# A transformer block on one core: VectorE's middle of a pass in another order, and one product moved from VectorE to GpSimd

## Chip, cores and metric

One core of a Trainium2 chip runs the kernel. The metric is the device time of one execution in microseconds (us). The engines are TensorE (PE, with PEld for its weight loads), VectorE (DVE), ScalarE (ACT), GpSimd (POOL) and SyncE (SP, which issues DMAs here). Each runs its own instructions in order and waits on semaphores for the others.

## What is computed

An attention block and a mixture-of-ranks block, each with a layer norm before and after, on x of 16 x 256 x 128 (float32):

```python
x = x + layernorm(attention(layernorm(x)))    # 2 heads of 64, half of each head rotated (rope)
x = x + layernorm(ffn(layernorm(x)))

def ffn(x):                                   # for each row of 128
    base = x @ W.T
    proj = l2norm(x @ Wp.T + bp)
    lw = softmax(proj @ l2norm(sim) * exp(min(temp, CLAMP_MAX)))       # 4 experts
    ret = where(arange(4) == argmax(lw), lw, 0.0)                      # the best expert's weight alone
    return base + sum(ret[e] * ((x @ Wd[e].T) @ Wu[e].T) for e in range(4))   # ranks 1, 2, 4, 8
```

## The kernel before

The 16 batches go through as 8 pairs, n = 0 to 7 (LAST = 7). A pair is four tiles of 128 rows (t = 0 to 3), and four units u (two batches by two heads) in attention. All of x stays in SBUF. The main loop is `for a in PASSES` with a = 0 to 6. A pass works on several pairs at once: the attention of pair a (names `now`), the projections of pair a+1 (`nxt`), the statistics of pair a+3 (`has(a + 3)`), the second half of attention and the second norm of pair a-1 (`last_`), and the routing and low-rank part of pair a-2 (`done`). Behind the loop stands a tail written out by hand, with pair 5 (LAST-2) and 6 (LAST-1) to be finished and pair 7 (LAST) in halves.

Each engine has its own block with its own copy of the loop, and the order of calls in it is written out by hand. Nothing plans it. So each engine's order is fixed, and a call that waits holds up everything behind it on its engine.

What the change and the steps of the prediction touch:

- DVE, statistics of pair a+3: `stats` (L643, four times), `gap` (L649, L650), `mean` (L654, L655), `variance` (L659). They feed `norm_rows` (L266) and `norm_shift` on POOL in the next pass. `normalise(a+2)` (L664) writes two of the four tiles that TensorE's `turn_x(a+2)` (L1322) transposes; ACT writes the other two.
- DVE, attention: `row_max` (L675) of a unit's scores in PSUM, `weights_sum` (L680), `add_head` (L688), `residual_y` (L695) with the factor `rsy` from POOL (L297; in the tail L319). The four residuals of pair a-1 release TensorE's `turn_x2(a-1)` (L1383). `add_head(a, 0, .)` frees the PSUM bank that `turn_probs(a, 3)` writes.
- DVE, second norm: `stats_2` (L701), `gap_2`, `square_2`, `variance_2` (L716). They feed POOL's `deviation` (L309), the standard deviation `std2`. `scaled_bias` (L721) multiplies it with the routing bias, 4 x 62 elements for each of 128 partitions. `add_bias` (L727) adds it to what TensorE's `project_z` (L1395) left in PSUM. POOL's `scaled_guards` (L312, L313) make the small limits that `length` (L744) reads.
- DVE, routing of pair a-2: `top_logit`, `square_sum`, `length`, `below_top`, `keys` (L752), `top_key`, `logits` (L761; it needs `inv_norm` from POOL), `is_top`, `shares` (L769; it needs `expert_exps` of ACT, L463), `pick`, `sum_exps`, `invert_sum`, `gates` (L787, L789), `gates_low` (L794). TensorE's `turn_gated` (L1403) and `low_rank` follow, then ACT's `variance_z` (L474), POOL's `factors_z` (L303, L305: `rsz`) and DVE's `residual_z` (L799).
- POOL, in a pass: `inverse_lengths`, `factors_y`, `norm_rows(a+2)`, `rope(a+1, 0)`, `norm_shift`, `factors_z(a-2)`, `deviation(a-1)`, `rope(a+1, 1)`, `scaled_guards(a-1)`. `rope` is three products and sums of 256 elements (L282, L285, L288). It releases TensorE's `turn_qk(a+1, 0)` and `turn_qk(a+1, 1)` (L1341). The second of these stands at the start of the next pass, behind `weigh(a, 3)`; but that of the last pair stands in pass 6, ahead of `weigh(6, 3)`:

```python
                if nxt:
                    scores(a + 1, 0, (x2t_out, a) if last_ else (probs_ready, 4 * a + 3))
                if a == LAST - 1:
                    turn_qk(LAST, 1, (y_ready, 4 * a + 3))
                if now:
                    weigh(a, 3)
```

- ACT: `exps` (L438) needs `row_max` and makes the probabilities that `turn_probs` (L1362) transposes; `scores(a, 1)` (L1352) waits for the first two; `probs_copy` (L444), `variance_y` (L449), `qkt_copy` (L433), which copies what `turn_qk` wrote, and `gated_copy` (L467).

Of the kernel before, what the change touches and what calls it, by code (L numbers as in the profile page):

```python
# [16 lines left out]
P = 128  # L17
# [26 lines left out]
def layer(nc, x, w_attn, vectors, w_ffn, w_down, sim, out):  # L44
# [3 lines left out]
    with ctx:  # L48
# [192 lines left out]
        def _(pool):  # L241
# [68 lines left out]

            def scaled_guards(n):
                pool.tensor_tensor(eps2[:, n % 2, :], ve2[:, :], eps[:, :], ALU.mult)  # L312
                pool.tensor_tensor(least2[:, n % 2, :], ve2[:, :], tiny[:, :], ALU.mult).then_inc(least_ready, 1)  # L313
# [34 lines left out]
            for a in PASSES:  # L348
                if has(a - 2):
                    inverse_lengths(a - 2)  # L350
                if has(a - 1):
                    factors_y(a - 1)
                if a == 0:
                    pool.wait_ge(post_link, 2)
                    pool.tensor_tensor(sim_n[:, :], sim_sq[:, :], power[0:PROJ, 0:EXPERTS], ALU.pow).then_inc(sim_norm, 1)
                if has(a + 2):
                    norm_rows(a + 2)
                if has(a + 1):
                    rope(a + 1, 0)
                if has(a + 2):  # L360
                    norm_shift(a + 2)
                if has(a - 2):
                    factors_z(a - 2)
                if has(a - 1):
                    deviation(a - 1)
                if has(a + 1):
                    rope(a + 1, 1)
                if has(a - 1):
                    scaled_guards(a - 1)
# [4 lines left out]
            deviation(LAST - 1)  # L374
            scaled_guards(LAST - 1)
# [13 lines left out]
        def _(act):  # L389
# [136 lines left out]
            for a in PASSES:  # L526
# [11 lines left out]
                if has(a - 1):  # L538
                    variance_y(a - 1, 1)
                if now:  # L540
                    exps(a, 1)
                if done:
                    expert_exps(a - 2)
# [73 lines left out]
        def _(dve):  # L617
# [101 lines left out]
            def scaled_bias(n):  # L719
                dve.wait_ge(std_ready, n + 1)  # L720
                dve.tensor_tensor(bias_s[:, :, :], bias_b[:, :].unsqueeze(1).to_broadcast([P, PT, RW]),  # L721
                                  std2[:, :].unsqueeze(2).to_broadcast([P, PT, RW]), ALU.mult).then_inc(scaled, 1)

# [35 lines left out]
            def logits(n):  # L759
                dve.wait_ge(inv_norm_ready, n + 1)  # L760
                dve.tensor_tensor(logit[:, :, :], below[:, :, :], rank_wide(inv_norm), ALU.mult).then_inc(logits_ready, 1)  # L761
# [306 lines left out]
            for a in PASSES:  # L1068
# [32 lines left out]
                if done:  # L1101
                    keys(a - 2)
                if has(a + 3):
                    stats(a + 3, 0)
                if done:
                    top_key(a - 2)
                    logits(a - 2)
                    is_top(a - 2)
                if has(a + 3):
                    stats(a + 3, 1)  # L1110
                    stats(a + 3, 2)
                if done:
                    shares(a - 2)
                    pick(a - 2)
                if has(a + 3):
                    stats(a + 3, 3)
                if done:
                    sum_exps(a - 2)
                if last_:
                    residual_y(a - 1, 0)  # L1120
                if done:
                    invert_sum(a - 2)
                if has(a + 3):
                    gap(a + 3)
                if done:
                    gates(a - 2)
                if has(a + 3):
                    mean(a + 3)
                if done:
                    gates_low(a - 2)  # L1130
                if has(a + 3):
                    variance(a + 3)
                if now:
                    row_max(a, 2)
                if last_:
                    residual_y(a - 1, 1)
                    residual_y(a - 1, 2)
                if now:
                    row_max(a, 3)
# [11 lines left out]
                if last_:  # L1151
                    residual_y(a - 1, 3)
# [12 lines left out]
                if last_:  # L1165
                    variance_2(a - 1)
                if done:
# [11 lines left out]
                if last_:  # L1179
                    scaled_bias(a - 1)  # L1180
# [51 lines left out]
            scaled_bias(LAST - 1)  # L1232
# [392 lines left out]
```

## Time and profile before

| | us |
|---|---|
| median of 3 runs | 150.67 (150.66 to 150.72) |
| the profiled execution | 150.58 |
| its span in the trace | 148.80 |
| TensorE busy | 128.5 (86%) |
| VectorE busy | 130.7 (88%) |
| ScalarE busy | 113.4 (76%) |
| GpSimd busy | 87.3 (59%) |

The page gives each engine's busy time, and then the chain of work that ended last: TensorE has 49% of it, VectorE 27%, ScalarE 15%. A group or a timeline row names the line of the kernel, the engine, the operation, output and inputs with their shapes, and how many instructions are merged in it. A bracket behind it is the idle time of the engine ahead of it and what ended that. PE instructions overlap, so the time that one takes in its engine is the distance of two starts.

### The profile page before, as it was taken

How to read it: one execution, taken by the hardware profiler on the slowest of the kernel's cores; microseconds unless marked ns; L12 is line 12 of the kernel's file. 1: busy time of each engine (PE TensorE's matmuls, PEld its weight loads, DVE VectorE, ACT ScalarE, POOL GpSimd, SP SyncE). 2: the span in 40 equal slices, each digit the busy share in tenths (PEclk: the TensorE clock that was granted, in tenths of full speed). 3: DMA queues.
4: the chain of work that ended last, by engine and by line, in shares of the span. 5: the costliest groups of instructions: out<-in, count | busy, mean ns of one | idle time of the engine just before them, and what ended most of it. 6: DMA issues, size and time to landing. Idle time of an engine off the chain costs nothing.

```text
span 148.8 us, 3110 instructions
## 1 busy us (share of the span) xinstructions
PE 128.5 (86%) x874; PEld 106.0 (71%) x874; DVE 130.7 (88%) x592; ACT 113.4 (76%) x378; POOL 87.3 (59%) x148
## 2 busy tenths in 40 slices
PE   0879799999999998999899989998999898965340
PEld 0467587988898788878887888797879776953220
DVE  6788879997988999899989998898889788899963
ACT  3657697969996989698969896989698958754460
POOL 6320826623846758676867686768545863338552
PEclk9999999999999999999999999999999999999555
DMA  3833250000000000100020002000200010000013
GB/s 74 209 98 92 74 134 5 4 0 0 7 0 2 0 0 4 70 0 2 4 73 0 0 0 75 0 0 0 73 4 2 9 62 0 4 0 2 0 70 141
DMA packets 5266, 4.83 MB, mean 32 GB/s; under 512 B 594, under 2 KB 5250, under 8 KB 5250
## 3 DMA queue, kind: packets, MB, share of 16 engines
q1 hardware_dynamic: 5104, 4.51, 10.4%
q8 instruction: 7, 0.11, 0.3%
q10 hardware_dynamic: 146, 0.13, 0.3%
q14 instruction: 9, 0.07, 0.2%
HBM read 2.54 MB, written 2.10 MB: 31 GB/s over the span
## 4 chain that ended last, share of the span: by engine, by line
PE 49%; DVE 27%; ACT 15%; issue 2%; POOL 2%; DMA 2%; POOLq 1%; DVEq 0%
PE ps_a L1372 6%; PE ps_s L1352 6%; ACT probs L438 6%; PE ps_z L1395 5%; PE ps_c L1372 4%; DVE neg_max L675 4%; PE ps_a L1362 4%; DVE x_all L695 3%; PE ps_b L1322 2%; PE ps_s L1383 2%; PE ps_s L1341 2%; PE ps_b L1362 2%; DVE y_all L688 2%; DMA x_all<-x 2%; PE ps_c L1341 2%
## 5 line engine op out<-in xcount | busy, mean ns | idle before, releaser
L438 ACT ACTIVATE probs<-ps_s,neg_max 128x256 f32<-128x256 f32 x60 | 25.3, 488 | 7.9 <-DVE neg_max L675 7.8
L675 DVE TENSOR_REDUCE neg_max<-ps_s 128x2 f32<-128x512 f32 x30 | 20.3, 680 | 0.6 <-PE ps_s L1352 0.4
L1352 PE MATMUL ps_s<-qk_t 64*128 64x256 f32 x120 | 17.0, 402 | 0.0
L1372 PE MATMUL ps_a<-v_all,probs_t 128*128 128x129 f32 x120 | 16.5, 280 | 0.0
L1372 PEld LDWEIGHTS ps_a<-v_all,probs_t 128*128 128x128 f32 x120 | 14.6, 191 | 2.0 <-issue 2.0
L1352 PEld LDWEIGHTS ps_s<-qk_t 64*128 64x128 f32 x120 | 10.3, 186 | 4.8 <-issue 4.0
L282 POOL TENSOR_TENSOR turn<-qk,sin_x 128x256 f32<-128x256 f32 x15 | 11.1, 740 | 3.1 <-ACT qk L424 2.2
L695 DVE SCALAR_TENSOR_TENSOR x_all<-y_all,rsy,x_all 128x128 f32<-128x128 f32 x32 | 11.8, 393 | 1.3 <-POOL rsy L297 0.7
L285 POOL TENSOR_TENSOR qk<-qk,cos_x 128x256 f32<-128x256 f32 x15 | 11.5, 767 | 1.2
L297 POOL TENSOR_TENSOR rsy<-var_y,power 128x4 f32<-128x4 f32 x6 | 6.5, 1078 | 9.3 <-ACT sq_y L449 9.3
L293 POOL TENSOR_TENSOR inv_norm<-norm,power 128x4 f32<-128x4 f32 x7 | 7.2, 1027 | 8.0 <-DVE norm L744 8.0
L288 POOL TENSOR_TENSOR qk<-qk,turn 128x256 f32<-128x256 f32 x15 | 10.9, 725 | 1.2
L266 POOL TENSOR_TENSOR rs<-ve,power 128x4 f32<-128x4 f32 x7 | 7.1, 1008 | 6.2 <-DVE ve L659 6.2
L449 ACT ACTIVATE sq_y<-y_all 128x129 f32<-128x129 f32 x32 | 10.1, 339 | 0.7 <-DVE y_all L688 0.6
L309 POOL TENSOR_TENSOR std<-ve,root 128x4 f32<-128x4 f32 x7 | 7.1, 1017 | 5.3 <-DVE ve L716 5.3
L1362 PE MATMUL ps_a<-ident,probs 128*128 128x128 f32 x60 | 9.1, 275 | 1.1 <-ACT probs L438 1.1
L444 ACT ACTIVATE probs_t<-ps_a 128x512 f32<-128x512 f32 x15 | 9.5, 637 | 0.5 <-PE ps_a L1362 0.5
L1395 PE MATMUL ps_z<-w_z,x_t 128*128 128x190 f32 x48 | 9.5, 325 | 0.0
L1362 PEld LDWEIGHTS ps_a<-ident,probs 128*128 128x128 f32 x60 | 7.0, 140 | 2.6 <-ACT probs L438 1.6
L1372 PE MATMUL ps_c<-v_all,probs_t 128*128 128x129 f32 x64 | 8.6, 278 | 0.2 <-ACT probs_t L444 0.2
L799 DVE SCALAR_TENSOR_TENSOR x_all<-ps_z,rsz,x_all 128x128 f32<-128x128 f32 x24 | 7.3, 342 | 1.4 <-POOL rsz L305 1.4
L1372 PE MATMUL ps_b<-v_all,probs_t 128*128 128x129 f32 x64 | 8.5, 276 | 0.0
(342 smaller groups left out, 442.0 us busy)
## 6 DMA issues: line engine op xcount, KB each, us to landing
x_all<-x SPq DMA_DIRECT2D x7, 256.0 KB, 2.8
out<-x_all SPq DMA_DIRECT2D x7, 256.0 KB, 2.1
x_all<-x SPq DMA_DIRECT2D x2, 128.0 KB, 2.7
out<-x_all SPq DMA_DIRECT2D x2, 128.0 KB, 1.7
w_raw<-w_attn ACTq DMA_DIRECT2D x1, 128.0 KB, 2.8
w_raw<-w_attn SPq DMA_DIRECT2D x1, 128.0 KB, 2.9
bo_bp<-vectors SPq DMA_DIRECT2D x1, 80.0 KB, 3.5
ffn_raw<-w_ffn SPq DMA_DIRECT2D x1, 71.5 KB
```

The source lines that it names most:

```text
L282: pool.tensor_tensor(turn[:, b, :, :, :], swapped, sin_x[:, :, :, :, :].rearrange("p t g h i -> p (t g) h i"), ALU.mult).then_inc(rope_mid, 1)
L285: pool.tensor_tensor(spatial, spatial, cos_x[:, :, :, :, :].rearrange("p t g h i -> p (t g) (h i)"), ALU.mult).then_inc(rope_mid, 1)
L288: pool.tensor_tensor(spatial, spatial, turn[:, b, :, :, :].rearrange("p g h i -> p g (h i)"), ALU.add).then_inc(rope_done, 1)
L438: last = act.activation(probs[:, u, j, :], scores_of(n, u)[:, j * T:(j + 1) * T], ACT.Exp, bias=neg_max[:, u, j:j + 1])
L444: act.activation(probs_t[:, u, :, :], unit_of(n, u)[:, :].rearrange("p (a t) -> p a t", a=TILES), ACT.Copy).then_inc(pt_out, 1)
L449: last = act.activation(sq_y[:, t, :], y_all[:, n * PT + t, :], ACT.Square, scale=E ** -0.5, accum_out=var_y[:, t:t + 1])
L675: dve.tensor_reduce(neg_max[:, u, :], scores_of(n, u)[:, :].rearrange("p (j k) -> p j k", j=TILES), AX.X, ALU.max, negate=True).then_inc(m ...
L695: dve.scalar_tensor_tensor(x_all[:, rows(n, t)], y_all[:, n * PT + t, 0:E], rsy[:, t:t + 1], x_all[:, rows(n, t)], ALU.mult, ALU.add).then ...
L1352: last = pe.matmul(scores_of(n, 2 * b + h)[:, j * T:(j + 1) * T], qk_t[r, b, 0, j * P:(j + 1) * P], qk_t[r, b, 1, :], start=True, stop=True)
L1362: last = pe.transpose(unit_of(n, u)[:, i * T + j * P:i * T + (j + 1) * P], probs[:, u, j, i * P:(i + 1) * P], ident[:, :])
L1372: last = pe.matmul(unit_of(n, u)[:, j * VW:(j + 1) * VW], probs_t[:, u, i, j * P:(j + 1) * P], v_all[:, at:at + VW], start=(i == 0), stop= ...
L1395: last = pe.matmul(z_of(n, k)[:, t, :], x2_t[:, 2 * k + t, :], w_z[:, :], start=(t == 0), stop=False, skip_group_check=True)
```

## The change

On POOL, `scaled_bias` is new: the same product, with `bias_s` as its output, behind `deviation`, in each pass from a = 1 and once in the tail. It waits for POOL's own `std_ready`, and for the `add_bias` of the pair before (`route_ready`), which read the tile. The same function and its two calls are gone from DVE. On ACT `expert_exps(a-2)` goes ahead of `exps(a, 1)`. On DVE the middle of a pass has another order: `logits` ahead of `keys`, the routing operations and the statistics interleaved otherwise, `row_max(a, 2)` and `row_max(a, 3)` next to each other, then `residual_y` 1, 2 and 3 of pair a-1 in a row, and `mean` and `variance` of pair a+3 behind `variance_2`, ahead of `residual_z` and `normalise`. TensorE's order stays as it is.

```diff
@@ GpSimd
+            def scaled_bias(n):
+                pool.wait_ge(std_ready, n + 1)
+                if n == 0:
+                    pool.wait_ge(post_dve, 5)
+                else:
+                    pool.wait_ge(route_ready, 2 * n)
+                pool.tensor_tensor(bias_s[:, :, :], bias_b[:, :].unsqueeze(1).to_broadcast([P, PT, RW]),
+                                   std2[:, :].unsqueeze(2).to_broadcast([P, PT, RW]), ALU.mult).then_inc(scaled, 1)
...
                 if has(a - 1):
                     deviation(a - 1)
+                    scaled_bias(a - 1)
                 if has(a + 1):
                     rope(a + 1, 1)
...
             deviation(LAST - 1)
+            scaled_bias(LAST - 1)
             scaled_guards(LAST - 1)
@@ ScalarE
+                if done:
+                    expert_exps(a - 2)
                 if now:
                     exps(a, 1)
-                if done:
-                    expert_exps(a - 2)
@@ VectorE
                 if done:
+                    logits(a - 2)
                     keys(a - 2)
                 if has(a + 3):
                     stats(a + 3, 0)
                 if done:
                     top_key(a - 2)
-                    logits(a - 2)
-                    is_top(a - 2)
                 if has(a + 3):
                     stats(a + 3, 1)
+                if done:
+                    is_top(a - 2)
+                    shares(a - 2)
+                if has(a + 3):
                     stats(a + 3, 2)
                 if done:
-                    shares(a - 2)
                     pick(a - 2)
+                    sum_exps(a - 2)
                 if has(a + 3):
                     stats(a + 3, 3)
                 if done:
-                    sum_exps(a - 2)
+                    invert_sum(a - 2)
                 if last_:
                     residual_y(a - 1, 0)
                 if done:
-                    invert_sum(a - 2)
+                    gates(a - 2)
                 if has(a + 3):
                     gap(a + 3)
                 if done:
-                    gates(a - 2)
-                if has(a + 3):
-                    mean(a + 3)
-                if done:
                     gates_low(a - 2)
-                if has(a + 3):
-                    variance(a + 3)
                 if now:
                     row_max(a, 2)
+                    row_max(a, 3)
                 if last_:
                     residual_y(a - 1, 1)
                     residual_y(a - 1, 2)
-                if now:
-                    row_max(a, 3)
+                    residual_y(a - 1, 3)
+                if now:
                     weights_sum(a, 0)
...
                 if last_:
-                    residual_y(a - 1, 3)
                     stats_2(a - 1, 2)
                     stats_2(a - 1, 3)
...
                 if last_:
                     variance_2(a - 1)
+                if has(a + 3):
+                    mean(a + 3)
+                    variance(a + 3)
                 if done:
                     residual_z(a - 2, 0)
...
-                if last_:
-                    scaled_bias(a - 1)
                 if now:
                     add_head(a, 2, 0)
...
             add_head(LAST, 2, 1)
-            scaled_bias(LAST - 1)
             weights_sum(LAST, 3)
```

## Rows read from the trace of the kernel before

**Rows 1.** Windows: a pass with statistics, one without; busy time of each engine, clock, DMA
```profile
60.79:75.70 14.91, 14.30 (x108) 12.18 (x106) 14.43 (x64) 12.96 (x46) 10.62 (x17) 1.00 0.06 19
90.60:105.44 14.84, 14.29 (x108) 12.17 (x106) 12.86 (x54) 12.90 (x46) 10.80 (x18) 1.00 0.06 20
```

**Rows 2.** Timeline of TensorE, pass 3: start, us, engine, line, operation, idle before
```profile
71.24 0.66 PE L1383 MATMUL ps_s<-ident,x_all 128*128 128x128 f32 x4 [0.61 <-DVE x_all L695]
```

**Rows 3.** Timeline of TensorE, pass 5: `turn_probs(2)`, `turn_x2`, `turn_probs(3)`
```profile
99.83 0.60 PE L1362 MATMUL ps_c<-ident,probs 128*128 128x128 f32 x4
100.27 0.60 PE L1383 MATMUL ps_s<-ident,x_all 128*128 128x128 f32 x4
101.41 0.66 PE L1362 MATMUL ps_a<-ident,probs 128*128 128x128 f32 x4 [0.55 <-ACT probs L438]
```

**Rows 4.** Timeline of POOL, pass 3: two of the three operations of `rope(4, 0)`
```profile
66.59 0.74 POOL L282 TENSOR_TENSOR turn<-qk,sin_x 128x256 f32<-128x256 f32 x1
67.40 0.74 POOL L285 TENSOR_TENSOR qk<-qk,cos_x 128x256 f32<-128x256 f32 x1
```

**Rows 5.** Timeline of DVE, pass 3: `mean`, `variance`; then all `mean` (ns: min/median/max)
```profile
66.62 0.73 DVE L654 SCALAR_TENSOR_TENSOR mean<-tmp,stats 128x4 f32<-128x4 f32 x1
...
67.47 0.69 DVE L659 SCALAR_TENSOR_TENSOR ve<-tmp 128x4 f32<-128x4 f32 x1
...
L654 DVE SCALAR_TENSOR_TENSOR mean<-tmp,stats x7: 165/168/726, 14.3 to 81.5; 128x4 f32<-128x4 f32 x7
```

**Rows 6.** Costliest groups: last sum of `rope`; then tile `bias_s` (ns: min/median/max)
```profile
L288 POOL TENSOR_TENSOR qk<-qk,turn 128x256 f32<-128x256 f32 x15 | 10.9, 725 | 1.2
...
L721 DVE TENSOR_TENSOR bias_s<-bias_b,std x7: 394/515/827, 44.0 to 130.8; 128x248 f32<-128x248 f32 x7
```

**Rows 7.** Timelines of POOL and DVE, start of pass 4: second guard, `length`
```profile
76.07 0.21 POOL L313 TENSOR_TENSOR least<-ve,tiny 128x4 f32<-128x4 f32 x1
...
77.21 0.15 DVE L744 TENSOR_TENSOR norm<-norm,least 128x4 f32<-128x4 f32 x1
```

**Rows 8.** Timelines, end of pass 6: `deviation`, last sum of `rope(7, 1)`, `turn_qk(7, 1)`, its copy
```profile
116.80 1.02 POOL L309 TENSOR_TENSOR std<-ve,root 128x4 f32<-128x4 f32 x1
...
119.46 0.72 POOL L288 TENSOR_TENSOR qk<-qk,turn 128x256 f32<-128x256 f32 x1
...
120.51 0.66 PE L1341 MATMUL ps_c<-ident,qk 128*128 128x128 f32 x4
...
121.21 0.60 ACT L433 ACTIVATE qk_t<-ps_c 128x512 f32<-128x512 f32 x1 [0.95 <-PE ps_c L1341]
```

**Rows 9.** Timelines of POOL and DVE, tail: `deviation(6)`, first operation of `gates(5)`
```profile
128.25 1.01 POOL L309 TENSOR_TENSOR std<-ve,root 128x4 f32<-128x4 f32 x1 [2.38 <-DVE ve L716]
...
129.78 0.22 DVE L787 TENSOR_TENSOR gate<-picked,total 128x60 f32<-128x60 f32 x1
```

**Rows 10.** Pass 0: `normalise(2)`, all of them; `rope(1, 1)`, first and last; `turn_x(2)`
```profile
28.66 1.38 DVE L664 TENSOR_SCALAR xn<-x_all,rs,nm 128x128 f32<-128x128 f32 x2
...
L664 DVE TENSOR_SCALAR xn<-x_all,rs,nm x12: 333/341/886, 28.7 to 102.8; 128x128 f32<-128x128 f32 x12
...
28.41 0.74 POOL L282 TENSOR_TENSOR turn<-qk,sin_x 128x256 f32<-128x256 f32 x1 [1.09 <-ACT qk L424]
...
30.04 0.72 POOL L288 TENSOR_TENSOR qk<-qk,turn 128x256 f32<-128x256 f32 x1
...
30.68 0.66 PE L1322 MATMUL ps_b<-ident,xn 128*128 128x128 f32 x4
```

**Rows 11.** Pass 1: TensorE's `turn_probs(2)`, `turn_x2`; DVE's `residual_y` 1 and 2
```profile
40.78 0.60 PE L1362 MATMUL ps_c<-ident,probs 128*128 128x128 f32 x4
41.41 0.66 PE L1383 MATMUL ps_s<-ident,x_all 128*128 128x128 f32 x4
...
38.45 1.08 DVE L695 SCALAR_TENSOR_TENSOR x_all<-y_all,rsy,x_all 128x128 f32<-128x128 f32 x2
```

**Rows 12.** Timeline of POOL, pass 1: `deviation(0)`
```profile
42.77 1.06 POOL L309 TENSOR_TENSOR std<-ve,root 128x4 f32<-128x4 f32 x1 [2.14 <-DVE ve L716]
```

More of the change, by code:

```diff
@@ L716, in variance_2 @@
                 dve.scalar_tensor_tensor(ve2[:, :], tmp2[:, 1, :], 1.0 / E, tmp2[:, 2, :], ALU.mult, ALU.add).then_inc(var2, 1)
[L719 to L722, printed above, removed]
             def add_bias(n, k):
@@ L760, in logits @@
                 dve.wait_ge(inv_norm_ready, n + 1)
+                dve.wait_ge(route_link, n * 9 + 3)
                 dve.tensor_tensor(logit[:, :, :], below[:, :, :], rank_wide(inv_norm), ALU.mult).then_inc(logits_ready, 1)
```

## The prediction

> **What bounds the kernel now.** I read the page first (the busy shares and the chain that ended last), then TensorE's timeline over two whole passes, then the timelines of VectorE (DVE), ScalarE (ACT) and GpSimd (POOL) beside it, and last the start, pass 1 and the tail, where the steady state doesn't hold. A pass (one value of a in the main loop) lasts 14.91 us where four more statistics, a mean and a variance lie in it (a = 2 to 4), and 14.84 us without them (a = 5) [rows 1]. TensorE is busy 14.30 and 14.29 us of these. So DVE's 14.43 busy us against 12.86 are worth only 0.07 us a pass: TensorE's order is the floor. In passes 2 to 4 TensorE waits 0.61 us for the last `residual_y` ahead of `turn_x2` [rows 2]. In pass 5 it doesn't: `turn_x2` follows `turn_probs(2)` after 0.44 us, and TensorE then waits 0.55 us for `exps(a, 3)` on ACT ahead of `turn_probs(3)` [rows 3]. ACT gets there from `gated_copy`, `exps(2)` and `variance_z`, all released by TensorE itself. Whoever frees DVE's middle finds this second wait behind the first.
>
> **DVE's middle (gain).** `mean` takes 0.73 us and `variance` 0.69 us in pass 3 and the median `mean` of all passes 0.17 [rows 5]. Both lie beside a product of `rope` on POOL and end with it: 66.59 + 0.74 = 67.33 against 66.62 + 0.73 = 67.35, and 67.40 + 0.74 = 68.14 against 67.47 + 0.69 = 68.16 [rows 4, 5]. Both read two SBUF operands. The change takes them out of the middle, joins the two maxima (PSUM operands, not held up) and puts `residual_y` 1 to 3 in a row behind. By these rows the middle loses about 1.2 us, and the last residual is ready about 1.1 us ahead of TensorE even if two of the three are held by a product of `rope`. The 0.61 us wait goes, the 0.55 us wait of pass 5 comes: a gain of 0.07 us in each of the passes 2, 3 and 4, **-0.21 us**. Passes 5 and 6 gain nothing. `logits` ahead of `keys` and `expert_exps` ahead of `exps(a, 1)` have one answer: `exps(a, 1)` ends some 0.2 us later, its reader `scores(a, 1)` has more slack than that, **0**. `mean` and `variance` at the end fall, in passes 2 to 4, into DVE's wait for `rsz`, beside a power on POOL: **0**. The cover is that wait, and pass 0 has none.
>
> The Trainium skill (SBUF — State Buffer, section "Who interferes with whom") says that a VectorE instruction with two SBUF inputs contends with a GpSimd instruction that reads SBUF, and that the later one fully blocks. By that rule, the trace agrees (the two ends above). It speaks for moving `mean` and against giving POOL one more product: without it the tail term below would lose 0.1 us and the pass 0 term would be 0.
>
> **The product on POOL (its price).** No POOL row has this shape (248 elements, both operands broadcast). The nearest is a product or sum of 256 elements, 725 ns in the mean over 15 [rows 6]: 0.70 us for 248, plus 0.08 us for the wait on POOL's own `std_ready` (the distance of dependent POOL instructions, as 66.59 + 0.74 to 67.40 [rows 4]): **0.78 us**. Bounds: 0.39 us, what DVE takes for it at the least, and 1.1 us, half as much again. On DVE 0.39 to 0.83 us go [rows 6], where it isn't late: in each pass and in the tail DVE waits next for TensorE's `project_z(., 1)`. So the removal alone is worth **0**. What is queued behind the product on POOL is `rope(a+1, 1)` and `scaled_guards(a-1)`; who waits for these is TensorE's `turn_qk(a+1, 1)` and DVE's `length`.
>
> In steady passes: the guards end at 76.07 + 0.21 = 76.28 and `length` reads them at 77.21 [rows 7]. They come at most 0.78 us later; POOL also starts `deviation` a little earlier (DVE's `variance_2` is earlier, so only `rsz` holds it): 0.15 to 0.4 us are left. **0**, with a cliff from about 1 us of product.
>
> In pass 6, the last, there is no such slack. `turn_qk(LAST, 1)` stands right behind `scores(LAST, 0)`, at 120.51, and `rope(LAST, 1)` ends at 119.46 + 0.72 = 120.18 [rows 8]. `deviation` starts there at 116.80 behind `rsz`, which ACT releases, so it can't be earlier. Now `rope` ends at 120.96, TensorE starts at 121.02 (0.06 us of a semaphore): **+0.51 us**. It is handed on: ACT has waited 0.95 us for just this operation [rows 8], the copy feeds `scores(LAST, 1)`, and the chain of waits runs from there over TensorE and ACT to the end without a gap of more than 0.3 us.
>
> In the tail the product runs from 128.25 + 1.01 + 0.08 = 129.34 to 130.04, and `gates` (two SBUF operands) comes at 129.78 [rows 9]; it ends at about 130.1 and not at 130.0, and the chain runs through it: **+0.1 us**.
>
> **Pass 0.** `mean(3)` and `variance(3)` now stand right ahead of `normalise(2)`, and `rope(1, 1)` runs beside it, from 28.41 to 30.04 + 0.72 = 30.76. There the two instructions of `normalise` together take 1.38 us, one of them 886 ns where the median is 341; so they too are held up by POOL [rows 10]. Now: `mean` is held to 29.15 by the first product; `variance`, 0.2 us behind, is held by the second to 29.96; the first `normalise` slips in between; the second is held by the third to about 30.9 instead of 30.04. TensorE's `turn_x(2)` stood at 30.68: **+0.28 us**. DVE itself, which has a short wait for TensorE behind, is about 0.6 us late, and so are the maxima and exponentials that open pass 1.
>
> **Pass 1.** Alone it would gain: `turn_x2` came 0.63 us behind `turn_probs(2)`, not 0.44 [rows 11], so -0.19. But DVE comes 0.6 us late; the second and third residual meet two products of `rope` (that pair took 1.08 us before [rows 11], with a maximum behind it), and now stand in a row ahead of `add_head(1, 0, .)`, which frees the bank for `turn_probs(3)`. I work that out to 42.2, where TensorE was free at 41.41 + 0.44 = 41.85. So passes 0 and 1 together: **+0.31 us** (an estimate, rounded down for the colder start that `turn_x2` had). `variance_2` is then 0.8 us later and `deviation` starts at 43.6 instead of 42.77 [rows 12]. In pass 6 `rope` ends 3.4 us behind the start of `deviation` (116.80 to 120.18 [rows 8]); with the product and two guards of 0.2 us that makes about 48.1 for the guards of pass 1. `length` of pass 2 would come two passes ahead of that in [rows 7], at 77.21 - 29.82 + 0.31 = 47.7. So DVE waits 0.4 us, and the copies on ACT hand perhaps 0.16 us of it to TensorE (bounds 0 and 0.4, taken low as the second exponential has slack): **+0.16 us**.
>
> **Sum.** -0.21 + 0.51 + 0.10 + 0.31 + 0.16 = +0.87 us on the profiled execution, 150.58 us (span 148.80), so 151.45; the median of the runs shown is 0.09 above it: 151.5 us, 0.6% slower.
>
> **Rivals.**
> 1. The start keeps its time (DVE's `normalise` finds a gap between POOL's products, or wins the second race). For it: instructions of this kind do slip between two products; against it: the 1.38 us of the pair there. Passes 0 and 1 give -0.19 and pass 2 nothing: -0.19 - 0.21 + 0.61 = +0.21, 150.9 us, within 0.2%. 20 in 100.
> 2. The faster side: POOL's product is cheap (near 0.39 us) or starts early, `rope(LAST, 1)` stays at most 0.1 us behind TensorE, and the start keeps its time: -0.40 + 0.2 = 150.5, down to 150.3 us with nothing left in the tail. It decides below 0.27 us of product and wait together (0.33 less a semaphore); no row speaks for that. 11 in 100.
> 3. The product takes 1.1 us or more on POOL: the tail pays 0.4 us more, and the guards come behind `length` in all of the passes 2 to 6, at up to 0.1 us each: 152.1 us. 12 in 100.
> 4. The change doesn't do what it says: `turn_x2` still waits for DVE in passes 2 to 4, as the three residuals are held longer than a product each. Then the -0.21 is missing: 151.7 us. 7 in 100, within the range of the forecast.
>
> The forecast has 50 in 100, from 151.2 to 151.8. About 0.2% (0.3 us) is what a measurement of this kernel can tell from no change. Slower by more than that (over 150.97): forecast, rivals 3 and 4 and a little of rival 1, 70 in 100. Within 0.2%: most of rival 1 and half of rival 2, 20. Faster: 10. The range of 8 in 10 leaves out the far end of rivals 2 and 3: 150.5 to 152.1.
>
> **What would show each step.** In the changed kernel: TensorE's wait ahead of `turn_x2` gone and 0.5 us ahead of `turn_probs(3)` in passes 2 to 4, which last 14.84 us; `mean` at 0.17 us there; POOL's new product at 0.70 us, 7 times; ACT's wait ahead of the copy for `scores(LAST, 1)` at 1.4 to 1.5 us instead of 0.95, with TensorE idle ahead of `turn_qk(LAST, 1)` for 0.5 us; in pass 0 `mean` and `variance` at 0.5 to 0.7 us and a wait ahead of `turn_x(2)`; in pass 2 POOL's guards behind DVE's `length`. The prediction is wrong if passes 2 to 4 come out shorter than 14.8 us, or if `turn_qk(LAST, 1)` isn't late.

## The result, and the profile after

The changed kernel takes 151.23 us (151.13 to 151.33) where the kernel before took 150.71 us (150.5 to 150.76) beside it on the same chip: ratio 1.0036, 95% interval 1.0027 to 1.0046. It is slower by 0.52 us. The profiled execution took 151.26 us, 0.68 us more than that of before.

The page after, parts 1 and 4 (busy time of each engine, then its share of the chain that ended last):

```profile
PE 129.2 (86%) x874; PEld 106.5 (71%) x874; DVE 128.9 (86%) x585; ACT 113.0 (76%) x378; POOL 90.0 (60%) x155
...
PE 57%; DVE 16%; ACT 15%; POOL 5%; issue 3%; DMA 2%; POOLq 1%; DVEq 0%
```

VectorE lost 1.8 us of busy time and went from 27% of the chain to 16%; POOL went from 87.3 to 90.0 us busy and now has 5% of the chain. Yet the kernel is slower.

One mark for each pass shows where: the start of `scores(a, 0)` on TensorE, the same instruction in both kernels (us from the start of the span).

| start of | before | after | pass lasts, before | after | difference |
|---|---|---|---|---|---|
| pass 0 | 15.31 | 15.45 | | | +0.14 (ahead of anything that was changed) |
| pass 1 | 31.27 | 31.69 | 15.96 | 16.24 | +0.28 |
| pass 2 | 45.49 | 46.03 | 14.22 | 14.34 | +0.12 |
| pass 3 | 60.41 | 60.86 | 14.92 | 14.83 | -0.09 |
| pass 4 | 75.32 | 75.69 | 14.91 | 14.83 | -0.08 |
| pass 5 | 90.22 | 90.52 | 14.90 | 14.83 | -0.07 |
| pass 6 | 105.06 | 105.36 | 14.84 | 14.84 | 0 |
| `scores(7, 0)` | 119.45 | 119.74 | 14.39 | 14.38 | -0.01 |
| `turn_qk(7, 1)` | 120.51 | 121.18 | 1.06 | 1.44 | +0.38 |

The column of differences adds up to +0.67 us, with 0.14 of it in the loading phase (in the experiments below this start lies between 15.10 and 15.51, whatever was changed); the rest agrees with the 0.52 us between the medians.

**The steady passes.** Windows of the kernel after, pass 3 and pass 5 (borders, length; busy time of PE, PEld, DVE, ACT, POOL; granted clock, DMA), to be laid beside [rows 1]:

```profile
60.86:75.69 14.83, 14.28 (x105) 12.16 (x104) 13.76 (x61) 12.92 (x46) 10.91 (x18) 1.00 0.06 19
90.52:105.36 14.84, 14.30 (x106) 12.17 (x105) 13.03 (x52) 12.93 (x46) 10.92 (x18) 1.00 0.05 18
```

VectorE has 0.67 us less to do in pass 3, and the pass is shorter by 0.08 us: the two kinds of pass are now alike. TensorE's timeline, pass 3, the three rows that answer to [rows 2, 3]:

```profile
70.46 0.60 PE L1366 MATMUL ps_c<-ident,probs 128*128 128x128 f32 x4
70.90 0.60 PE L1387 MATMUL ps_s<-ident,x_all 128*128 128x128 f32 x4
...
72.05 0.66 PE L1366 MATMUL ps_a<-ident,probs 128*128 128x128 f32 x4 [0.55 <-ACT probs L449]
```

`turn_x2` follows `turn_probs(2)` after 0.44 us without a wait, and the wait is in its new place, 0.55 us for `exps(3)`.

**Pass 0.** Timelines of VectorE, POOL and TensorE after, to be laid beside [rows 10]:

```profile
28.80 0.52 DVE L665 SCALAR_TENSOR_TENSOR mean<-tmp,stats 128x4 f32<-128x4 f32 x1
29.42 0.70 DVE L670 SCALAR_TENSOR_TENSOR ve<-tmp 128x4 f32<-128x4 f32 x1
30.04 1.00 DVE L675 TENSOR_SCALAR xn<-x_all,rs,nm 128x128 f32<-128x128 f32 x2
...
28.55 0.74 POOL L282 TENSOR_TENSOR turn<-qk,sin_x 128x256 f32<-128x256 f32 x1 [1.10 <-ACT qk L435]
29.37 0.73 POOL L285 TENSOR_TENSOR qk<-qk,cos_x 128x256 f32<-128x256 f32 x1
30.18 0.78 POOL L288 TENSOR_TENSOR qk<-qk,turn 128x256 f32<-128x256 f32 x1
...
31.10 0.66 PE L1326 MATMUL ps_b<-ident,xn 128*128 128x128 f32 x4 [0.22 <-DVE xn L675]
```

Each operation of `rope` holds one step of VectorE, which ends only with it: `mean` ends at 29.32 with the first (28.55 + 0.74 = 29.29), `variance` at 30.12 with the second (30.10), `normalise` at 31.04 with the third (30.96). TensorE then waits 0.22 us.

**The end of pass 6.** Timelines of POOL and TensorE, then ACT, to be laid beside [rows 8]:

```profile
117.14 1.01 POOL L309 TENSOR_TENSOR std<-ve,root 128x4 f32<-128x4 f32 x1
118.23 0.60 POOL L317 TENSOR_TENSOR bias_s<-bias_b,std 128x248 f32<-128x248 f32 x1
...
120.40 0.72 POOL L288 TENSOR_TENSOR qk<-qk,turn 128x256 f32<-128x256 f32 x1
...
121.18 0.66 PE L1345 MATMUL ps_c<-ident,qk 128*128 128x128 f32 x4 [0.30 <-POOL qk L288]
...
121.87 0.60 ACT L444 ACTIVATE qk_t<-ps_c 128x512 f32<-128x512 f32 x1 [1.32 <-PE ps_c L1345]
```

TensorE now waits for POOL ahead of `turn_qk(7, 1)`, and ACT's wait behind it grew from 0.95 to 1.32 us. In the chain of waits POOL stands here from `std` to `qk` without a break.

### The profile page after: what moved, and what is told of

Read it like the earlier page. It is cut to its first block, busy times and chain, and to the rows that moved or that the text cites. A ratio compares the mean times of both kernels' runs of the same rounds, so it can differ in the third digit from the quotient of the medians.

```text
span 149.5 us, 3124 instructions
## 1 busy us (share of the span) xinstructions
PE 129.2 (86%) x874; PEld 106.5 (71%) x874; DVE 128.9 (86%) x585; ACT 113.0 (76%) x378; POOL 90.0 (60%) x155
## 4 chain that ended last, share of the span: by engine, by line
PE 57%; DVE 16%; ACT 15%; POOL 5%; issue 3%; DMA 2%; POOLq 1%; DVEq 0%
PE ps_a L1376 10%; PE ps_s L1356 9%; ACT probs L449 5%; PE ps_z L1399 4%; PE ps_a L1366 4%; ACT sq_z L485 3%; PE ps_b L1366 3%; PE ps_c L1376 3%; PE ps_c L1345 3%; PE ps_b L1326 2%; DMA x_all<-x 2%; DVE y_all L699 2%; PE ps_s L1345 1%; ACT gated_t L478 1%; PE ps_d L1333 1%
## 5 line engine op out<-in xcount | busy, mean ns | idle before, releaser
L686 DVE TENSOR_REDUCE neg_max<-ps_s 128x2 f32<-128x512 f32 x30 | 19.8, 683 | 1.6 <-PE ps_s L1356 1.4
L706 DVE SCALAR_TENSOR_TENSOR x_all<-y_all,rsy,x_all 128x128 f32<-128x128 f32 x32 | 13.5, 460 | 1.5 <-POOL rsy L328 0.8
L285 POOL TENSOR_TENSOR qk<-qk,cos_x 128x256 f32<-128x256 f32 x15 | 10.9, 730 | 1.2
```

What stands on the lines that cost most here:

```text
L285: pool.tensor_tensor(spatial, spatial, cos_x[:, :, :, :, :].rearrange("p t g h i -> p (t g) (h i)"), ALU.mult).then_inc(rope_mid, 1)
L686: dve.tensor_reduce(neg_max[:, u, :], scores_of(n, u)[:, :].rearrange("p (j k) -> p j k", j=TILES), AX.X, ALU.max, negate=True).then_inc(m ...
L706: dve.scalar_tensor_tensor(x_all[:, rows(n, t)], y_all[:, n * PT + t, 0:E], rsy[:, t:t + 1], x_all[:, rows(n, t)], ALU.mult, ALU.add).then ...
```

## The experiments

The theory is the prediction's: the reordering gains in the passes 1 to 4 and loses in pass 0 (and hands it to pass 1), and the product on POOL costs in the pass with no slack, pass 6. Against it stand, first, that the loss has one cause alone (the reordering, or POOL's queue in every pass), and second, that one wait is only exchanged for another, so that a repair of one place moves nothing. Each expectation says which it tells apart; a later question is how the gain of the steady passes comes about.

**1. The reordering alone.** The product is back on VectorE, the rest is the change.

```diff
@@ the changed kernel, GpSimd
-                    scaled_bias(a - 1)
...
@@ VectorE
...
+                if last_:
+                    scaled_bias(a - 1)
                 if now:
                     add_head(a, 2, 0)
...
```

> The new order on DVE and ACT alone; the product of deviation and routing bias stays on DVE, where the kernel before has it. Theory A (three places that add up: the start, where mean and variance meet rope ahead of normalise, +0.28 us in pass 0 and +0.12 in pass 1; passes 2 to 4, -0.08 each; the tail, +0.38 through the late rope of the last pair): +0.28 + 0.12 - 0.24 = +0.16 us over the kernel before, 150.87 us, and turn_qk(LAST, 1) not late. Theory B (the product on POOL is the whole loss, the order only gains): -0.4 to -0.25 us. Theory C (the order is the whole loss): +0.5 us.

Measured: 150.90 us, ratio 1.0015 (1.0006 to 1.0024), +0.25 us. In its trace the starts of the passes lie at 15.44, 31.66, 45.99, 60.81, 75.64, 90.46, 105.29 and 119.67, those of the full change within 0.07 us, but `turn_qk(7, 1)` comes 1.07 us behind the last of them, without a wait. TensorE's timeline, pass 6:

```profile
120.74 0.66 PE L1342 MATMUL ps_c<-ident,qk 128*128 128x128 f32 x4
```

So the loss of the start belongs to the reordering alone, and the loss of the end doesn't.

**2. The product on POOL alone**, in the order of before.

```diff
@@ the kernel before, GpSimd
                     deviation(a - 1)
+                    scaled_bias(a - 1)
...
@@ VectorE
...
-                if last_:
-                    scaled_bias(a - 1)
...
```

> The product on POOL alone; the order on DVE and ACT as before. Theory A: the tail's +0.38 us and nothing in pass 0; pass 1 and 2 at most 0.1 more, as variance_2 isn't late there: +0.4 us, 151.1 us. Theory B: +0.5 us or more, spread over the passes. Theory C: 0.

Measured: 151.08 us, ratio 1.0029 (1.0018 to 1.0041), +0.43 us. The starts of the passes (15.10, 31.11, 45.34, 60.22, 75.12, 90.02, 104.85, 119.23) give passes of 14.88 to 14.90 us with statistics, as before. The loss is at the end, 1.39 us from `scores(7, 0)` to

```profile
120.62 0.66 PE L1344 MATMUL ps_c<-ident,qk 128*128 128x128 f32 x4 [0.25 <-POOL qk L288]
```

The two parts alone add up to 0.68 us, the whole costs 0.52; the intervals of the two (about 0.15 us each) leave room for that.

**3. The product on VectorE in pass 6 only.** Undoes one call of the change.

```diff
@@ the changed kernel, GpSimd
-                    scaled_bias(a - 1)
+                    if a != LAST - 1:
+                        scaled_bias(a - 1)
@@ VectorE
...
+                if a == LAST - 1:
+                    scaled_bias(a - 1)
                 if now:
                     add_head(a, 2, 0)
```

> The changed kernel with the product back on DVE in pass 6 alone (6 of 7 products stay on POOL). Theory A: rope(LAST, 1) is on time, turn_qk(LAST, 1) follows scores(LAST, 0) without a wait, and 0.38 of the 0.52 us lost are back: +0.15 us over the kernel before, 150.85 us. Theory B (POOL's load in every pass): a sixth or a seventh of the loss comes back, under 0.1 us. Theory C: nothing comes back.

Measured: 150.83 us, ratio 1.0011 (1.0002 to 1.0020). Of the seven products on POOL this one cost 0.4 us (1.0036 less 1.0011, times 150.7), what `turn_qk(7, 1)` was late by; it now stands 1.07 us behind `scores(7, 0)` (119.73), without a wait:

```profile
120.80 0.66 PE L1353 MATMUL ps_c<-ident,qk 128*128 128x128 f32 x4
```

**4. `mean` and `variance` in the middle in pass 0 only.**

```diff
@@ the changed kernel, VectorE
                 if has(a + 3):
                     gap(a + 3)
+                if a == 0:
+                    mean(a + 3)
+                    variance(a + 3)
...
-                if has(a + 3):
+                if has(a + 3) and a > 0:
                     mean(a + 3)
                     variance(a + 3)
```

> The changed kernel with mean(3) and variance(3) of pass 0 back in the middle, behind gap(3); all later passes as changed. Theory A: normalise(2) is on time, turn_x(2) waits for nothing (-0.28 us), DVE isn't late in pass 1, turn_x2 is released in time there and the wait that the kernel before had goes (-0.3 us): 0.6 us under the changed kernel, 150.65 us, -0.05 us against the kernel before. Theory B: no change against the changed kernel (+0.5). Theory C (the order in the passes, wherever it stands): under 0.1 us comes back.

Measured: 150.62 us, ratio 0.9996 (0.9987 to 1.0004). Starts at 15.31, 31.23, 45.27, 60.10, 74.93, 89.75, 104.57, 118.96: pass 0 lasts 15.92 us, pass 1 14.04, together 0.62 us less than after the full change. So the place of two small instructions in one pass costs 0.6 us. VectorE and TensorE, pass 0:

```profile
28.66 1.35 DVE L675 TENSOR_SCALAR xn<-x_all,rs,nm 128x128 f32<-128x128 f32 x2
...
30.65 0.66 PE L1329 MATMUL ps_b<-ident,xn 128*128 128x128 f32 x4
```

`normalise` meets the products of `rope` as it did before ([rows 10]), and TensorE doesn't wait. Pass 1 also shows the gain that the late start had covered: 14.04 against 14.22 us before.

**5. Both repairs** (3 and 4 in one kernel).

> The changed kernel with both repairs: the product of pass 6 back on DVE, and mean(3) and variance(3) of pass 0 back in the middle. Theory A: the two losses are separate and add up: 0.4 us under the kernel with the second repair alone, 0.4 us under the kernel before, 150.25 us (ratio 0.997). If the two share a cause (both are POOL being late somewhere), less than 0.2 us comes on top of the better one of them.

Measured: 150.24 us, ratio 0.9973 (0.9964 to 0.9983), faster than before by 0.36 us. The starts from pass 2 on (45.27, 60.10, 74.93, 89.75, 104.58, 118.97) are those of experiment 4 within 0.01 us, so the two repairs don't touch each other. Neither wait was only exchanged for another: what each cost comes back whole.

**6. The product of pass 6 twice**, the first into a tile that is free then. It adds a product and takes nothing away.

```diff
@@ the changed kernel, GpSimd
                     deviation(a - 1)
+                    if a == LAST - 1:
+                        pool.wait_ge(std_ready, a)
+                        pool.tensor_tensor(bias_e[:, :, :], bias_b[:, :].unsqueeze(1).to_broadcast([P, PT, RW]),
+                                           std2[:, :].unsqueeze(2).to_broadcast([P, PT, RW]), ALU.mult)
                     scaled_bias(a - 1)
```

> The changed kernel with the product done twice on POOL in pass 6 alone (the first into a tile that is written anew later). Theory A: POOL's time ahead of rope(LAST, 1) goes to the end one for one: another 0.6 us, +1.1 us over the kernel before, 151.8 us; TensorE waits 0.9 us ahead of turn_qk(LAST, 1). If the 0.38 us were something else than this wait (the lock on DVE, ACT's late exponentials), under 0.2 us more.

Measured: 151.69 us, ratio 1.0070 (1.0057 to 1.0083). Against the changed kernel +0.5 us, and TensorE's wait went from 0.30 to 0.85 us, by about one product of 0.60:

```profile
121.48 0.66 PE L1349 MATMUL ps_c<-ident,qk 128*128 128x128 f32 x4 [0.85 <-POOL qk L288]
```

At this place each product on POOL goes straight to the end of the kernel.

**7. `mean` and `variance` at the end, nothing else** (from pass 1 on). This was to show the 0.07 us of the passes 2 to 4 alone, and the two held instructions as their cause.

```diff
@@ the kernel before, VectorE
                 if has(a + 3):
                     gap(a + 3)
...
-                if has(a + 3):
+                if a == 0:
                     mean(a + 3)
...
-                if has(a + 3):
+                if a == 0:
                     variance(a + 3)
...
                 if last_:
                     variance_2(a - 1)
+                if has(a + 3) and a > 0:
+                    mean(a + 3)
+                    variance(a + 3)
```

> The kernel before with one edit: from pass 1 on, mean and variance stand behind variance_2. No other reordering, no product on POOL. Theory A: the two held instructions are the whole of what keeps the last residual_y from TensorE, so this alone gives pass 1 its 0.2 us and passes 2 to 4 their 0.08 us each: -0.4 us, 150.25 us. Rival: the gain needs the maxima together and the three residuals in a row as well: -0.1 us at most.

A miss, with the sign wrong: 151.16 us, ratio 1.0035 (1.0023 to 1.0048). The passes 2 to 4 last 15.1 us (starts 45.69, 60.80, 75.93, 91.07), longer than before. VectorE's timeline, pass 3, with TensorE's `turn_x2` and `turn_x` and POOL's `rope` beside it:

```profile
67.14 0.66 DVE L794 TENSOR_TENSOR gated<-gate,gated 128x60 fp32r<-128x60 f32 x1
...
68.32 1.16 DVE L695 SCALAR_TENSOR_TENSOR x_all<-y_all,rsy,x_all 128x128 f32<-128x128 f32 x2
...
71.37 0.66 PE L1386 MATMUL ps_s<-ident,x_all 128*128 128x128 f32 x4 [0.36 <-DVE x_all L695]
...
74.57 0.66 PE L1325 MATMUL ps_b<-ident,xn 128*128 128x128 f32 x4
...
73.43 1.08 DVE L664 TENSOR_SCALAR xn<-x_all,rs,nm 128x128 f32<-128x128 f32 x2
...
73.71 0.72 POOL L282 TENSOR_TENSOR turn<-qk,sin_x 128x256 f32<-128x256 f32 x1
```

Most of the time that `mean` and `variance` were held stayed in the middle. `gates_low`, which took their place beside `rope`, now takes 0.66 us instead of 0.21, and two residuals 1.16 us instead of 0.67: that is 0.94 of the 1.2 us. The rest did arrive: the last residual ends 10.51 us after the start of the pass (71.31), where it ended 10.77 us after it before (71.18), and `turn_x2` waits for it for 0.36 us instead of 0.61. So the 0.2 us a pass were not lost in the middle but at the new place. There the two stand ahead of `residual_z` and `normalise`, though `rsz` is ready (at 72.58, before `variance` starts at 72.83), and they push `normalise` onto the next `rope`, beside which its pair takes 1.08 us (twice its 333 to 341 ns is 0.68, [rows 10]). It ends at 74.51, and TensorE's `turn_x`, which needs it, starts at 74.57.

**8. The maxima and residuals joined, nothing else.** This one is the opposite part: `mean` and `variance` stay where they were held.

```diff
@@ the kernel before, VectorE
                     row_max(a, 2)
+                    row_max(a, 3)
                 if last_:
                     residual_y(a - 1, 1)
                     residual_y(a - 1, 2)
+                    residual_y(a - 1, 3)
                 if now:
-                    row_max(a, 3)
                     weights_sum(a, 0)
...
                 if last_:
-                    residual_y(a - 1, 3)
                     stats_2(a - 1, 2)
```

> The kernel before with only the maxima joined and the three residuals in a row; mean and variance stay in the middle, held at 0.7 us each. Theory D: the held time costs nothing by itself as long as the last residual isn't behind the heads: it ends at about 70.1 in the clock of the trace of before, TensorE wants it at 70.5, so passes 2 to 4 fall to 14.84 us and the whole to 150.3 us (-0.3). Theory A (the two held instructions are the delay): the 1.2 us are still there, -0.1 us at most.

Measured: 150.29 us, ratio 0.9971 (0.9960 to 0.9982). A few moved lines of one engine beat both kernels, by 0.4 us the kernel before. The passes 2 to 5 last 14.82, 14.82, 14.83 and 14.82 us (starts 45.42, 60.24, 75.06, 89.89, 104.71), and pass 1 14.05 instead of 14.22. VectorE's timeline, pass 3, then TensorE's:

```profile
66.46 0.73 DVE L654 SCALAR_TENSOR_TENSOR mean<-tmp,stats 128x4 f32<-128x4 f32 x1
...
67.31 0.68 DVE L659 SCALAR_TENSOR_TENSOR ve<-tmp 128x4 f32<-128x4 f32 x1
67.92 1.28 DVE L675 TENSOR_REDUCE neg_max<-ps_s 128x2 f32<-128x512 f32 x2
69.11 0.86 DVE L695 SCALAR_TENSOR_TENSOR x_all<-y_all,rsy,x_all 128x128 f32<-128x128 f32 x3
...
70.28 0.60 PE L1383 MATMUL ps_s<-ident,x_all 128*128 128x128 f32 x4
...
71.42 0.66 PE L1362 MATMUL ps_a<-ident,probs 128*128 128x128 f32 x4 [0.54 <-ACT probs L438]
```

`mean` and `variance` are held just as before, 0.73 and 0.68 us, and it costs nothing: the last residual is ready at 69.97, 0.3 us ahead of TensorE. In the changed kernel it is ready at 69.82, 1.08 us ahead of TensorE (70.90), and the pass is no shorter: a residual that is in time gains nothing by being earlier. What made `turn_x2` wait in the kernel before is that the third residual stood behind a maximum and the first heads, not that the middle held two blocked instructions.

**9. `mean` and `variance` moved, maxima joined**, the product still on VectorE and the routing operations in the order of before; in pass 0 the two stay in the middle.

> The kernel with mean and variance moved alone (from pass 1 on), and now also row_max 2 and 3 next to each other and residual_y 1, 2 and 3 in a row behind them. Gates' chain, logits and expert_exps as in the kernel before, products on DVE. New theory D (what holds DVE is the run of three products of rope, whoever reads two SBUF operands then; what counts is that PSUM reads stand beside it and that the last residual comes ahead of the heads): turn_x2 in time, passes 2 to 4 at 14.84 us, -0.4 us, 150.2 us. Theory A': the gates' chain pulled forward is needed too: no gain against the kernel before, or a loss as with mean moved alone (+0.5).

Measured: 150.40 us, ratio 0.9977 (0.9968 to 0.9986), passes 14.82 and 14.83 us. No gain beyond experiment 8: with the residuals in a row, the place of `mean` is worth nothing, as its end is hidden either way.

**10. The whole reordering, no product on POOL, pass 0 repaired.** This asks what the product on POOL is worth where it does no harm.

> The new order with mean(3) and variance(3) of pass 0 in the middle, and every product on DVE as in the kernel before. Theory A: moving the product to POOL buys nothing in any pass, so this is as fast as the kernel with both repairs, 150.25 us, within 0.1 us. Rival: DVE's 0.4 us a pass, which the move frees, are worth something: slower than that kernel by 0.2 us or more.

Measured: 150.25 us, ratio 0.9974 (0.9962 to 0.9985), against 150.24 with six of the seven products on POOL (experiment 5). VectorE's relief is worth nothing, as the prediction had it.

**11. The second wait removed too.** On the kernel of experiment 10 ACT's `exps(a, 3)` goes ahead of `variance_z(a-2)`.

```diff
@@ the kernel of experiment 10, ScalarE
                     exps(a, 2)
-                if done:
-                    variance_z(a - 2)
                 if now:
                     exps(a, 3)
+                if done:
+                    variance_z(a - 2)
```

> The new order with every product on DVE and mean(3) in the middle of pass 0, and one more edit on ACT: exps(a, 3) ahead of variance_z(a-2), so that TensorE's 0.55 us wait ahead of turn_probs(3) goes. If that wait is what bounds passes 2 to 6, each gains up to 0.5 us (-2 us, 148 us). But variance_z comes 0.7 us later, and with it rsz, deviation, the product, add_bias and the guards: I expect DVE and POOL to be late next at the end of the pass, and 0.1 to 0.3 us a pass to be left: 149.0 us, 148.3 to 150.3.

A miss: 152.15 us, ratio 1.0097 (1.0081 to 1.0112), with passes of 15.12 to 15.16 us. The wait of 0.55 us is gone, and a longer way has opened. The chain of waits of this kernel, pass 3 (start, us, what):

```profile
70.69 1.04 ACT sq_z L474 x8
...
71.80 0.23 POOL var_z L303
...
72.09 1.03 POOL rsz L305
...
73.15 0.62 DVE x_all L800 x2
...
73.81 0.91 PE ps_z L1399 x4
```

`project_z(a-1, 0)` writes the bank that `residual_z(a-2)` reads, and that one needs `rsz`, for which `variance_z` is the start. The order on ACT was the right one of the two; the 0.55 us are not to be had by this exchange.

**12. A probe of the hold**, run once: the changed kernel with three tiny instructions (four elements or one) between the maxima and the residuals of each pass: a reduce of one tile, a product of two tiles, a reduce. It adds work, so its time says nothing.

```diff
@@ the changed kernel, VectorE
                     row_max(a, 3)
+                    dve.tensor_reduce(probe[:, 0, 0:1], eps[:, :], AX.X, ALU.add)
+                    dve.tensor_tensor(probe[:, 1, :], eps[:, :], one[:, :], ALU.mult)
+                    dve.tensor_reduce(probe[:, 2, 0:1], eps[:, :], AX.X, ALU.add)
...
```

> The changed kernel with three small instructions on DVE behind row_max(a, 3), where rope(a+1, 0) runs on POOL: a sum over one SBUF operand, a product of two SBUF operands, a sum over one again, 4 elements each. If two SBUF operands are what is held: the sums take 0.1 to 0.2 us in all passes, the product up to 0.7 us where a product of rope runs. If any DVE access to SBUF is held, the first sum is.

Measured: 151.16 us. The groups of the tile `probe` (ns: min/median/max), then VectorE's and POOL's timelines in pass 1:

```profile
L1141 DVE TENSOR_REDUCE probe<-eps x7: 144/146/148, 25.8 to 112.7; 128x1 f32<-128x4 f32 x7
L1142 DVE TENSOR_TENSOR probe<-eps,one x7: 151/216/402, 25.9 to 112.8; 128x4 f32<-128x4 f32 x7
L1143 DVE TENSOR_REDUCE probe<-eps x7: 143/143/147, 25.9 to 112.9; 128x1 f32<-128x4 f32 x7
...
39.47 0.40 DVE L1142 TENSOR_TENSOR probe<-eps,one 128x4 f32<-128x4 f32 x1
...
39.12 0.73 POOL L286 TENSOR_TENSOR qk<-qk,cos_x 128x256 f32<-128x256 f32 x1
```

A reduce of one tile is not held in any of the seven passes (147 or 148 ns at most); a product of two tiles of the same size is, until the product on POOL ends (39.47 + 0.40 = 39.87 against 39.12 + 0.73 = 39.85).

The Trainium skill (SBUF — State Buffer, section "Who interferes with whom") says this for the chip: a reduce never contends, a VectorE instruction with two SBUF inputs does contend with a GpSimd instruction that reads SBUF, and the later one waits for the whole of the other. For `rope` this trace agrees, with the numbers above. For POOL's powers of four elements the traces don't: VectorE's `mean` and `variance` of the changed kernel, pass 3, read two SBUF operands each beside the power that makes `rsz` and take as long as alone.

```profile
71.62 1.06 POOL L305 TENSOR_TENSOR rsz<-var_z,power 128x4 f32<-128x4 f32 x1
...
72.04 0.15 DVE L665 SCALAR_TENSOR_TENSOR mean<-tmp,stats 128x4 f32<-128x4 f32 x1
...
72.31 0.16 DVE L670 SCALAR_TENSOR_TENSOR ve<-tmp 128x4 f32<-128x4 f32 x1
```

So their new place holds nothing up in the changed kernel, as the prediction had it ("beside a power on POOL: 0").

## Why the prediction was right, and where it was not

It said 151.5 us in a range of 150.5 to 152.1, slower; it came to 151.23 us, slower by 0.52 us, at the low edge of the forecast's own case (151.2 to 151.8). Its sum was +0.87 us on the profiled execution, and 0.68 was measured there, 0.14 of it ahead of anything changed. Step by step:

- **Passes 2 to 4, -0.07 us each: right in size, wrong in part in its reason.** They gained 0.09, 0.08 and 0.07, and the wait for `exps(3)` took over with 0.55 us. But the step read the hold of `mean` and `variance` [rows 4, 5] as time to be gained by moving them. Experiment 7 moved them alone: the last residual came 0.26 us earlier and not 1.2, and the new place cost more than that. Experiment 8 left them held and had the whole gain. The cause is the place of the last residual. The sentence that the rule "speaks for moving `mean`" falls with it. The 0 for the new place was right in the changed kernel, where VectorE still waits 0.25 us for `rsz` behind the two; in experiment 7 that wait, the cover that the step named, was gone.
- **Pass 0, +0.28 us: right.** Each hold came as it was worked out (`mean` to 29.32, `variance` to 30.12, second `normalise` to 31.04; all 0.14 to 0.17 us later than written, as the whole span was 0.14 later). Net +0.28; experiment 4 takes it back.
- **Pass 1, +0.03 us of the +0.31: it was +0.12.** Experiment 4 splits it: the gain of 0.18 (forecast 0.19) is there, and the late start costs 0.30. The step priced one wait, for the bank that `add_head(1, 0, .)` frees, at 0.35 us; it came, at 0.14 (`turn_probs(3)` stands 0.59 us behind `turn_x2`, in experiment 4 0.45). It put at nothing the other, which is as large: the late maxima and exponentials that open pass 1 also hold up `scores(1, 1)`, which starts 5.60 us after the start of the pass instead of 5.44 (ACT's `exps(1, 1)` ends at 37.15, `scores(1, 1)` starts at 37.29). So passes 0 and 1 cost 0.40 us.
- **Pass 2, +0.16 us for `length` behind the guards: it didn't come.** The guards end at 47.98 (47.78 + 0.20) and `length` starts at 48.02. The two lines:

```profile
47.78 0.20 POOL L322 TENSOR_TENSOR least<-ve,tiny 128x4 f32<-128x4 f32 x1
...
48.02 0.16 DVE L750 TENSOR_TENSOR norm<-norm,least 128x4 f32<-128x4 f32 x1
```

  The maximum ahead of `length` ended at 48.01, so of the 0.4 us of waiting worked out at most 0.1 is left, and pass 2 was 0.09 us shorter than before. Experiment 1, without the product on POOL, settles it: there the guards end at 47.33, `length` starts at 47.98 all the same, and pass 2 lasts 14.82 us. Both ends were off: with the 0.14 us of the later start added to what was written, the guards came 0.26 us early (47.98, not 48.24) and VectorE 0.18 us late (48.02, not 47.84). `deviation(0)` started at 43.67, as forecast (43.6), but the product behind it took 0.60 us, not 0.70. This was the term with the longest chain of assumptions, three rows moved over two passes, and it met a difference no larger than their errors.
- **The guards in the steady passes, 0: right.** In pass 4 they end at 76.96 and `length` starts at 77.60.
- **The product, 0.70 us and 0.08 for its wait: 0.60 and 0.08.** All seven, the tile's group after (ns: min/median/max):

```profile
L317 POOL TENSOR_TENSOR bias_s<-bias_b,std x7: 600/602/603, 44.8 to 129.8; 128x248 f32<-128x248 f32 x7
```

  It is 117.14 to 118.23 from `deviation` to the product, 1.01 + 0.08. The estimate by the row of `rope` was 0.1 us too long.
- **The end of pass 6, +0.51 us: +0.38.** The mechanism is shown by experiments 3 (taken away: -0.4 us of the kernel's time) and 6 (doubled: TensorE's wait +0.55). The term was too large by the 0.1 us of the product.
- **`gates` behind the product in the tail, +0.1 us: 0.** The product ends at 130.43, and `gates` starts at 130.45 and takes 0.22 us, as long as before [rows 9]. From `turn_qk(7, 1)` to `turn_gated` both kernels take 10.49 us. With 0.70 us of product the two would have met.

```profile
129.83 0.60 POOL L317 TENSOR_TENSOR bias_s<-bias_b,std 128x248 f32<-128x248 f32 x1
...
130.45 0.22 DVE L794 TENSOR_TENSOR gate<-picked,total 128x60 f32<-128x60 f32 x1
```

- **The relief of VectorE, 0: right** (experiments 5 and 10). One wait was not foreseen: in pass 1 `add_bias` waits 0.44 us for POOL's product (45.41). It costs nothing: pass 1 lasts 14.33 us in experiment 1, where VectorE makes the product itself, and 14.34 with it on POOL.

Of the 0.19 us between the sum (0.87) and the ledger (0.68), the pieces are: start jitter +0.14, pass 1 +0.09, pass 2 -0.16 (and 0.02 more gained there), end of pass 6 -0.13, tail -0.10. Without the late start, which belongs to no step, the sum was 0.87 where the kernel lost 0.53 us (0.52 between the medians). But for pass 1 every term that erred was too large. The two large losses (the start and the end of pass 6) and the sign were right, two small ones (pass 2 and the tail) never came, and the whole loss was forecast more than half too high.

The passes 2 to 5 lasted 14.82 to 14.84 us in every kernel with the residuals in a row, but for experiment 11. What is left there is TensorE's own work (14.3 us busy) and the 0.55 us for `exps(3)`.

Not tried: the joined residuals of experiment 8 together with other changes to the tail, and the pass 0 loss with `rope(1, 1)` moved instead of `mean`. Which of its shape or its broadcast operands makes POOL's product of 248 elements cheaper than that of 256 was not taken apart either.

## What to carry to other kernels

An instruction that is held by another engine shows the time of the holder: before it is moved, look at what comes into its place, since the next instruction with two SBUF operands took most of the hold over here (0.94 of 1.2 us), and a maximum from PSUM did not. A step put into an engine's queue costs what is queued behind it in the one pass with the least slack, and that is rarely a steady one: here six of seven products were free, and the last cost 0.4 us; two small instructions were harmless in the passes with a wait to hide them, cost 0.6 us in the first, and 0.2 us in each pass of experiment 7, where VectorE was later and the wait gone. When the thing that ends last is one instruction (`turn_x2`'s last residual), move that one: it gave the whole gain, and a large reordering around it gave no more.

## What the hardware showed

- On POOL a product of 248 elements with both operands broadcast took 0.600 to 0.603 us, a product of 256 without broadcast, in `rope`, 0.72 to 0.74 us where VectorE didn't hold it: some 0.13 us apart for 8 elements.
- VectorE's `normalise`, with one SBUF tensor as input and SBUF as output, is held beside `rope` too (1.35 us for a pair in pass 0 of experiment 4, 1.08 in experiment 7, as in [rows 10]), where the probe's reduce never was.
- POOL is held by VectorE as well: beside the residuals of experiment 12 (from 39.86 on) the third operation of `rope` took 0.85 us instead of 0.73.

```profile
39.86 1.33 DVE L707 SCALAR_TENSOR_TENSOR x_all<-y_all,rsy,x_all 128x128 f32<-128x128 f32 x3
...
39.93 0.85 POOL L289 TENSOR_TENSOR qk<-qk,turn 128x256 f32<-128x256 f32 x1
```

- Between two products of `rope` lie 0.08 us (28.55 + 0.74 to 29.37 in pass 0), and a VectorE instruction can slip in there: the first `normalise` of pass 0 ran its course between the second operation of `rope` and the hold by the third. It would explain why each hold takes one instruction of a row and not all; this is argued from the ends above and was not isolated.
